# GpSimd's scatters in runs of three calls in place of four

## The reference, cut to what matters

```python
x = x + q * scan(sigmoid(a), kv)      # q, kv, a = rmsnorm(layernorm(x)) @ w_qkva.T; the scan runs along the tokens
h = layernorm(x)                      # 8192 tokens, taken as 8 groups of 1024
raw = softmax(h @ router_w)           # 8 experts; the two largest of a token are chosen
slot = position of the token among those of its group with the same expert, dropped from 256 on
out = gate1 * ffn[e1](h) + gate2 * ffn[e2](h)   # ffn = (gelu(h @ w0) * (h @ w1)) @ wo, width 1368
return x + out
```

## Time and profile before

| | us |
|---|---|
| runs, unprofiled | 1636.42, 1638.04, 1643.01 |
| the profiled execution, its own time | 1645.42 |
| its span (what the trace covers) | 1643.70 |
| PE busy | 1605.5 (98% of the span) |
| DVE busy | 920.3 |
| ACT busy | 765.1 |
| POOL busy | 501.5 |

### The profile page before, as it was taken

One profiled execution on the slowest core, in us unless ns is written; L12 is line 12 of the kernel. 1 busy time (PEld: TensorE's weight loads), 2 busy tenths in 40 slices (PEclk: granted clock), 3 DMA queues, 4 the chain that ended last, 5 costly groups with the idle time before them and its releaser, 6 DMA issues.

```text
span 1643.7 us, 22949 instructions
## 1 busy us (share of the span) xinstructions
PE 1605.5 (98%) x8522; PEld 1373.0 (84%) x8522; DVE 920.3 (56%) x1804; ACT 765.1 (47%) x1405; POOL 501.5 (31%) x433
## 2 busy tenths in 40 slices
PE   7999989899999999999999999999999999999998
PEld 6877778788888888888888888888888888888887
DVE  7998754346644564446544654465445644465442
ACT  5866645334433453445443543354334533454343
POOL 2256566652222222222222222222222222222111
PEclk9999999999999999999999999999999999999999
DMA  7554121035322342234222521253224422342111
GB/s 170 167 150 129 54 80 46 12 53 131 63 39 40 85 92 38 37 67 104 36 36 37 129 46 36 40 118 63 40 39 85 92 40 36 72 105 33 32 14 14
DMA packets 193848, 110.94 MB, mean 67 GB/s; under 512 B 96008, under 2 KB 189640, under 8 KB 193736
## 3 DMA queue, kind: packets, MB, share of 16 engines
q1 hardware_dynamic: 165064, 75.37, 18.3%
q0 software_dynamic: 28672, 34.10, 12.8%
HBM read 60.11 MB, written 34.61 MB: 58 GB/s over the span
## 4 chain that ended last, share of the span: by engine, by line
PE 87%; DVE 3%; POOL 2%; ACT 2%; issue 2%; DMA 2%; another core or an unknown queue 2%; SPq 1%; POOLq 0%; DVEq 0%; ACTq 0%
PE bank L1687 26%; PE bank L1710 23%; PE bank L1726 17%; PE bank L1728 9%; PE bank L1485 6%; PE bank L1701 2%; PE bank L1526 1%; POOL out L732 1%; POOL slots L664 1%; PE bank L1501 1%; SPq L518 1%; PE bank L1514 1%; DVE y L1428 1%; ACT hhi L942 0%
## 5 line engine op out<-in xcount | busy, mean ns | idle before, releaser
L732 POOL DMA_INDIRECT out<-xring,slot_records x128 | 213.3, 1666 | 848.0 <-DVE xring L1398 782.9
L942 ACT ACTIVATE hhi<-y 128x512 fp32r<-128x512 f32 (+1 forms) x349 | 220.4, 631 | 505.2 <-DVE y L1428 418.0
L1726 PE MATMUL bank<-wo,hhi 128*128 128x512 f32 (+1 forms) x1276 | 442.7, 384 | 0.2 <-DVE hlo L1431 0.2
L1428 DVE TENSOR_TENSOR y<-bank,sig 128x512 f32<-128x512 f32 x320 | 220.9, 690 | 326.2 <-PE bank L1710 293.0
L1728 PE MATMUL bank<-wo,hlo 128*128 128x256 f32 x1396 | 382.1, 274 | 0.1
L1431 DVE TENSOR_TENSOR hlo<-y,hhi 128x512 fp32r<-128x512 f32 (+1 forms) x349 | 241.8, 693 | 243.5 <-ACT hhi L942 236.5
L932 ACT ACTIVATE sig<-bank 128x512 f32<-128x512 f32 x320 | 189.6, 592 | 192.1 <-PE bank L1687 173.4
L1726 PEld LDWEIGHTS bank<-wo,hhi 128*128 128x128 f32 (+1 forms) x1276 | 239.1, 187 | 47.1 <-DVE hlo L1431 0.5
L1728 PEld LDWEIGHTS bank<-wo,hlo 128*128 128x128 f32 x1396 | 261.5, 187 | 9.2 <-issue 0.8
L1687 PE MATMUL bank<-xThi,whi 128*128 128x512 f32 (+1 forms) x704 | 216.5, 389 | 6.6 <-ACT sig L932 3.7
L1687 PE MATMUL bank<-xTlo,whi 128*128 128x512 f32 (+1 forms) x704 | 212.7, 383 | 0.0
(11 more groups left out here) (140 smaller groups left out, 1676.5 us busy)
## 6 DMA issues: line engine op xcount, KB each, us to landing
stage<-in_L_ffn_w_kernel SPq DMA_DIRECT2D x160, 128.0 KB
rows<-rows SPq DMA_DIRECT2D x448, 32.0 KB, 1.9
stage<-in_L_ffn_wo_kernel SPq DMA_DIRECT2D x80, 128.0 KB
xring<-in_L_attn_x SPq DMA_DIRECT2D x16, 512.0 KB
out<-xring SPq DMA_DIRECT2D x16, 512.0 KB
x_rows<-rows SPq DMA_DIRECT2D x16, 512.0 KB
slots<-records,sloti POOLq DMA_INDIRECT x128
rows<-x_rows,slot_records POOLq DMA_INDIRECT x128
```

The costliest lines, as they stand in the source:

```text
L732: pool.indirect_dma_start(out_rows, bass.IndirectOffsetOnAxis(idx, 0), ysb[:, t % 2, j, :], None, compute_op=ALU.add).then_inc(added, 16)
L942: act.activation(h_high(e, t, hc)[0:n, :], hf[0:n, hc % 2, :], ACT.Copy).then_inc(h_hi, 1)
L1428: dve.tensor_tensor(hf[0:n, hc % 2, :], up_value(e, t, hc)[0:n, :], gel[0:n, hc % 2, :], ALU.mult).then_inc(mul_done, 1)
L1726: pe.matmul(lines(yb[j][:, :]), high, lines(wo[0:n, hc, :, :].rearrange("p s c -> p (s c)")), start=hc == 0, stop=end, skip_group_check=True)
```

## The change

Scatters are counted in calls, not in pairs. The wait for a landing stands before each call whose number is a multiple of three (`RUN = 3`), wherever the call to `scatter` began. In steps 3 to 6 the twelve calls are placed three, six and three around the powers, in step 7 and behind the pipeline nine and fifteen (eight and sixteen before), in expert 0 three before `gather(0, 2)` and 29 behind it. The number of calls, what each writes and the order of calls among themselves stay. `landed` now waits for exactly the call named.

```diff
+    RUN = 3
-            def landed(n):
-                g, t = divmod(n, TILES)
-                pool.wait_ge(scattered[t // HT][g % 2], SCATTERED * (g // 2) + 16 * 2 * (t % HT + 1))
+            def landed(c):
+                g, t, k = c // (2 * TILES), c // 2 % TILES, c % 2
+                pool.wait_ge(scattered[t // HT][g % 2], SCATTERED * (g // 2) + 16 * (2 * (t % HT) + k + 1))
             def scatter(a, b):
-                for n in range(a, b):
-                    g, t = Turn(n // TILES), n % TILES
-                    if n == 0:
+                for c in range(a, b):
+                    g, t, k = Turn(c // (2 * TILES)), c // 2 % TILES, c % 2
+                    if c == 0:
                         pool.wait_ge(emptied, 16 * 2 * FT)
-                    elif (n - a) % 2 == 0:
-                        landed(n - 1)
-                    if t == 0:
+                    elif c % RUN == 0:
+                        landed(c - 1)
+                    if t == 0 and k == 0:
                         wait(pool, routed, g, 1, 1)
-                    for k in range(2):
-                        pool.indirect_dma_start(
...
+                    pool.indirect_dma_start(
...
-            PER_STEP = 6
-            left = PER_STEP * (G - 4) + 12
+            PER_STEP = 12
+            left = PER_STEP * (G - 4) + 24
...
                 if i.value == G - 1:
                     gather(0, 0)
                     powers2(i.plus(-1), 0)
-                    scatter(n, n + 4)
+                    scatter(n, n + 9)
                     powers2(i.plus(-1), 1)
-                    scatter(n + 4, left)
+                    scatter(n + 9, left)
                     return
                 if n >= 0:
-                    scatter(n, n + 2)
+                    scatter(n, n + 3)
                 if A:
                     powers1(i.plus(1))
                 if C:
                     powers2(i.plus(-1), 0)
                 if n >= 0:
-                    scatter(n + 2, n + 4)
+                    scatter(n + 3, n + 9)
                 if C:
                     powers2(i.plus(-1), 1)
                 if n >= 0:
-                    scatter(n + 4, n + 6)
+                    scatter(n + 9, n + 12)
...
-            late = TILES * (G - 2)
+            late = 2 * TILES * (G - 2)
...
-            scatter(left, left + 4)
+            scatter(left, left + 9)
             powers2(last_group, 1)
-            scatter(left + 4, late)
+            scatter(left + 9, late)
...
-                        scatter(late, late + 2)
+                        scatter(late, late + 3)
...
-                        scatter(late + 2, TILES * G)
+                        scatter(late + 3, 2 * TILES * G)
```

More of the change, by code:

```diff
@@ L646, in powers2 @@
                 pool.tensor_tensor(sc2[:, h, :], ve2[:, h, :], halves[:, 0, :], ALU.pow).then_inc(pow2, 1)
-            def landed(n):
-                g, t = divmod(n, TILES)
-                pool.wait_ge(scattered[t // HT][g % 2], SCATTERED * (g // 2) + 16 * 2 * (t % HT + 1))
+            def landed(c):
+                g, t, k = c // (2 * TILES), c // 2 % TILES, c % 2
+                pool.wait_ge(scattered[t // HT][g % 2], SCATTERED * (g // 2) + 16 * (2 * (t % HT) + k + 1))
             def scatter(a, b):
-                for n in range(a, b):
-                    g, t = Turn(n // TILES), n % TILES
-                    if n == 0:
+                for c in range(a, b):
+                    g, t, k = Turn(c // (2 * TILES)), c // 2 % TILES, c % 2
+                    if c == 0:
                         pool.wait_ge(emptied, 16 * 2 * FT)
-                    elif (n - a) % 2 == 0:
-                        landed(n - 1)
-                    if t == 0:
+                    elif c % RUN == 0:
+                        landed(c - 1)
+                    if t == 0 and k == 0:
                         wait(pool, routed, g, 1, 1)
-                    for k in range(2):
-                        pool.indirect_dma_start(
-                            slots[:, :], bass.IndirectOffsetOnAxis(sloti[:, g.ring(RING), k, t:t + 1], 0),
-                            records[:, g.ring(RING), k, t, :], None).then_inc(scattered[t // HT][g.parity], 16)
+                    pool.indirect_dma_start(
+                        slots[:, :], bass.IndirectOffsetOnAxis(sloti[:, g.ring(RING), k, t:t + 1], 0),
+                        records[:, g.ring(RING), k, t, :], None).then_inc(scattered[t // HT][g.parity], 16)
             def gather(e, t):
```

## The result

The changed kernel takes 1648.41 us (median of seven runs, 1646.45 to 1651.89), the kernel before 1639.98 in seven runs beside it (1636.42 to 1643.01): ratio 1.006, 95% interval 1.0046 to 1.0074. It is 8.4 us slower by the medians; 5.7 were forecast. The profiled execution of the changed kernel took 1649.99 us, its span is 1648.2.

What follows compares the result with a forecast made beforehand. PE, busy 1605.5 of 1643.7 us, bounds the kernel; POOL's lateness reaches it through expert 1's weights. Eight more waits at 1.10 less 3.08 give 5.7 on the median 1638.04: 1643.7 us, own range 1641 to 1646, overall 1637 to 1648.5.

Steps and rivals of the forecast that it cites:

- The durations: POOL's scatters: 1.26 us a call, and 1.10 us for each added quiet wait for a landing.
- +2.36 us: Step 7, `powers2` of half 1: one more call (+1.26) and wait (+1.10) move it from 203.73 to 206.09.
- Steps 3 to 6: nothing: Steps 3 to 6: the new placement and waits are hidden by DVE's order; cost taken as 0.
- within 1 us, hidden: SP's first `load_records(0, 0)`, waiting for call 31: delay within 1 us, hidden by PE's and ACT's own order.
- Of the lateness 3.08 us are swallowed: At call 112, which had stood 3.38 us for DVE's routing: that wait absorbs 3.08 us, +3.5 left.
- The sum: Last scatter +5.72 us, from eight more waits at 1.10 less 3.08, laid on the median 1638.04: 1643.7 us.
- PE's 0.4 us behind ACT's 2.98: Expert 0's last tile: ACT waits 2.98 us for expert 1's weights, PE loses only 0.4 us behind it.
- The stand that I had at about 3.0 us: PE before expert 1's weights: weights 5.7 us later, PE itself already 3.1 late, so it stands about 3.0 us.
- (a): PE at half clock behind its 3.0 us stand before expert 1's weights: 1.7 us more, 1645.4 us; chance 20%.
- (b): Steps 3 to 6: the wait inside the run of six meets traffic, powers late; 1647.6 to 1648.9 us; chance 13%.
- (c): Not slower: runs of three land by themselves, waits cost nothing, PE gains 0.4 us: 1637.6 us; chance 12%.
- (d): Faster: runs of three may break up the 10.75 us without known releaser at 290.06, but nothing arrives; chance 3%.

Runs made afterwards that it cites:

- the kernel before with early weights: Kernel before, but SP issues the first four pieces of expert 1's weights before expert 0: 1633.87 us, ratio 0.996 on chip 9.
- the kernel with runs of eight late: Kernel before with landing waits every eighth instead of fourth call from call 48 on: 1631.12 us, 0.994 on chip 9; 1677.84 us, 1.017 on chip 12.
- the pair with early weights: Kernel before and changed kernel, both issuing expert 1's first four weight pieces before expert 0: 1633.87 us (0.996) and 1644.46 us (1.0026), chip 9.
- the steps alone: Steps 3 to 6 as in the changed kernel, calls from 48 on as in the kernel before: 1646.48 us (1.0001) and 1648.06 us (0.9996).
- late calls alone: Steps 3 to 6 as in the kernel before, calls from 48 on as in the changed kernel: 1653.68 us (1.0039) and 1653.37 us (1.0035).
- the kernel with the placement alone: Placement of the changed kernel, but waits at multiples of four as in the kernel before: 1655.20 us, ratio 1.0047 on chip 12.

## Why the prediction was wrong

**The durations held.** Before `powers2` of half 1 of step 7 I had +2.36 us. From the powers of half 0 to those of half 1 it is 15.22 us in the changed kernel and 12.29 in the kernel before with early weights: +2.9. DVE, which I had 1.47 us late there, waited 1.76 us. Between 185 and 345 us there are 24 landing waits of 36.6 us in the changed kernel, 16 of 25.8 in the profile before: 10.8 us more idle, less 8 x 0.30 that a call has anyway, is 8.4 for eight waits, 1.05 each against 1.10. This average holds waits in traffic and covered ones in both; a quiet wait was 1.39 to 1.41. The Trainium skill ("DMA: Bandwidth & Descriptors", anatomy of one DMA, SWDGE path), by whose 2.0 us a wait would be 0.74, is further off.

**"Steps 3 to 6: nothing" failed.** I wrote that SP's first `load_records(0, 0)` is "within 1 us, hidden". Call 31 is the fifth of six with a landing wait ahead (3.07 us); SP issues the load at 147.37 and the next load of x at 150.78, DVE gets x at 155.93 after 5.58 us, PE stands 4.88 us before 159.15. SP and DVE of the changed kernel:

```profile
147.37 0.33 SPq L559 DMA_DIRECT2D slot_records<-slots  x1
...
150.78 0.37 SPq L471 DMA_DIRECT2D xring<-in_L_attn_x  x1
```

```profile
155.93 0.75 DVE L994 BATCH_NORM_STATS2 st<-xring 128x6 f32<-128x256 f32 x2 [5.58 <-DMA xring<-in_L_attn_x]
```

In the kernel with runs of eight late, whose steps are those of before, on chip 9:

```profile
146.03 0.33 SPq L559 DMA_DIRECT2D slot_records<-slots  x1
...
149.46 0.37 SPq L471 DMA_DIRECT2D xring<-in_L_attn_x  x1
```

```profile
157.37 0.68 PE L1485 MATMUL bank<-xThi,wThi 128*128 128x512 f32 x2 [2.04 <-DVE y L1037]
```

1.3 us later at SP, 1.8 later at PE. Of PE's 4.2 us more idle time in the steps, in the pair with early weights, 4.67 - 2.15 = 2.5 are at this place. Beyond that PE has one wait of 2.88 us (127.93 above) behind a power that DVE had waited 2.88 us for, and its other, smaller waits sum to less. In the changed kernel itself the largest of that kind was 1.31, and DVE's waits for powers in steps 3 to 6 sum to 2.2 us, less than the 2.8 in the kernel before with early weights. Together the powers of step 7 are at 188.84 and 189.28 in the changed kernels without stalls, at 186.04 and 186.49 in those with the old steps: +2.8 us at the start of POOL's late stretch, and 4.2 us of PE. These are readings of profiles: the steps alone were never timed where there are no stalls. Where there are stalls they came out even twice (0.9996, 1.0001). ACT has waits of 2.3 to 2.7 us with the releaser "remote" at 111.9 and 138.6 in the first profile of before, beside eight calls with only powers between them, and none there in the changed kernel's second profile, where there are six; so the change may take away about what it adds. That was not tried.

**"Of the lateness 3.08 us are swallowed" failed.** Call 112's wait for DVE's routing is no fixed part of the kernel before. With stalls it is there in three of five profiles (3.38, 4.81 and 3.40 us; in the other two call 112 waits 1.39 and 1.40 for the landing before it). Without stalls it isn't: call 112 waits 1.40 for the landing in the kernel before with early weights, at 301.52, and 1.39 with runs of eight, even at 298.63. That DVE's stand at 290 made the routing late is likely by this, and not shown. Without the routing's wait call 112 has a landing wait of its own in the kernel before, so that the change adds seven waits, 7 x 1.10 = 7.70: from the powers of half 0 to the last scatter it is 146.04 us in the changed kernel (334.88 - 188.84), 138.36 in the kernel before with early weights (324.40 - 186.04), +7.7 where the forecast had 5.72. With the 2.8 of the steps the last scatter is 10.5 us late. How 10.5 us there become 8.4 at the end isn't worked out. The reload of 4.70 us and the half clock add to it, and waits that PE has anyway (5.4 us in the kernel before, by its gain from early weights) take off. In the pair with early weights, where these weights are out of the chain, PE meets the same lateness at the rows and at the moved pieces, and the difference is 10.6.

**The sum was put on the wrong base.** I saw that the profiled execution was 7.4 us above the median and laid the step on the median all the same. By the later profiles the 7.4 us were not noise but stalls: the kernel before takes 1647 to 1648 us where it shows them. Both of the forecast's credits (call 112's wait, and PE's 0.4 us behind ACT's 2.98) were taken from the profile with stalls; without them the first was not there, and PE's wait was worth 5.4 us. The stand that I had at about 3.0 us was 12.73. Where the stalls are, the forecast's size holds: late calls alone 6.4 and 5.8 us (ratios 1.0039 and 1.0035 times the median of before), the whole change 4.6 (1.0028), against 5.7.

**The rivals.** (a) happened (20% given): its 1.7 us was 1.8. (b) happened in small part (13% given): its wait in traffic came (3.01 and 3.07 us inside two of the four runs of six), but DVE's waits for powers in the steps were no longer in sum, and the larger part of PE's added waits in the steps (2.5 of 4.2 us) was SP's hold, which (b) did not contain. Its mechanism is plain in the kernel with the placement alone. (c) is out: behind `gather(0, 2)` no wait of the changed kernel's profile was under 1.39 us. (d) named the 10.75 us at 290 and asked if runs of three break that up. They don't at that place (9.43 us in the changed kernel's second profile), perhaps in part elsewhere: the waits without a releaser sum to 32.8 us there, to 44 to 58 in the five profiles of the kernel before. Where there are stalls the whole change was measured at 1.0028 and its late part alone at 1.0035 and 1.0039, with overlapping intervals. A gain over 0.5% there was not. `gather(0, 2)` was forecast at 287.7 and came at 283.08 because its start, the powers of half 0, was 2.6 us earlier without the stall and its 284.52 in the earlier trace rows held the stalls: in the kernel before with early weights it is at 277.41. Counted from the powers it moved by 94.24 - 91.37 = 2.9 us, against 3.14.

**Open.** What the steps and the late calls cost apart from each other where there are no stalls. Why the last landing and reload take 4.7 to 5.4 us in some executions (4.70, 4.99 and 5.38 in the changed kernel and the one with early weights, 4.87 with the late calls alone, 4.75 with the placement alone) and 3.0 to 3.3 in others with the same late calls. What stops DVE, ACT and PE while POOL issues. One candidate was not tried: between 204 and 240 us the profile's DMA queues move one packet of instructions in the stalled kernel of chip 12 and three in the same kernel on chip 9, and whether that is a cause or only follows from the engines standing the traces don't tell. Whether the kernel before with early weights, 0.4% faster than before on chip 9, keeps that where there are stalls: it was not run there. Runs of eight are no improvement to take, since they gain 0.6% on one chip and lose 1.7% on another.

## What to carry to other kernels

When the profiled execution is outside the timed runs, find out which idle times make up the difference before anything is summed: a cover that stands behind such a stall may be missing in the runs that count. A wait added on one engine must be followed through each queue that waits for the calls behind it, with the others' loads that stand behind in that queue. And place landing waits where something else already separates the calls: the same period with the old placement cost 1.3% instead of 0.6%. Waiting every eighth call instead of every fourth cost 29.6 us on one chip and gained 8.1 on another.

## What was not expected of the hardware

During long series of DMA calls issued by GpSimd the other engines stood still, on some chips and not on another. With eighteen and twelve of POOL's instructions in a row, DVE stood 8.63 and 14.91 us, up to 1.1 and 0.3 us before the series ended. ACT stood 7.93 us in the midst of the second, and PE 6.80, 6.26 and 5.84 us, the last until 3.9 us after its end; on chip 9 the same kernel had none of it. In the kernel before it happens with series of nine and twelve. The landing waits in this kernel, which look like pure loss (1.05 us each), break the series. The cause isn't shown: the profile knows no releaser.

With other traffic about, POOL stood 2.70 to 6.36 us for a landing instead of 1.40. During the 6.36 (152 to 159 us) the DMA engines were busy 79% of the time and moved 239 GB/s; at a quiet wait (206 to 210 us) it was 3% and 3 GB/s. As POOL's idle time goes, (6.36 - 0.30) / 1.10 = 5.5 quiet waits.

PE's granted clock fell to 0.53 behind a stand of 12.73 us and was back at 1.00 within 4 us, much as behind the stand of 2.60 us in the earlier trace rows (0.51 for 3.41 us): the long stand cost 1.8 us by the clock and the short one 1.7. The Trainium skill ("TensorE: Matmul & The Clock Gate", Part 1) has an idle PE at half its clock; the trace agrees.
